# Second cross attention: TensorE takes a column's edge (x, result, logits, coefficients) between the projections and the attention's turn, instead of at the column's end

## The reference, cut to what matters

```python
def _L1_xattn_ref(q, k, v, Wq, Wk, Wv, Wo):     # 16 heads of 8 features, k = ctx_1024
    qp = q @ Wq.T
    kp = k @ Wk.T
    score = jnp.einsum('bldn,bmdn->blmn', qh, kh) / jnp.sqrt(jnp.float32(HEAD_DIM))
    attn = jax.nn.softmax(score, axis=2)
    x = jnp.einsum('blmn,bmdn->bldn', attn, kh)     # the keys serve as values
    return x.reshape(b, l, DIM) @ Wo.T

def _route(x, router_w, e_bias):                # first step of the experts' block
    scores = jax.nn.sigmoid(x @ router_w.T)
    sfc = scores + e_bias[None, :]
    ...                                         # the 4 best of 8 groups, in them the 8 best experts
    w = jnp.take_along_axis(scores, topk_idx, axis=1)
    w = w / (w.sum(-1, keepdims=True) + 1e-20)
    return (topk_idx, w * SCALE)

x = _layernorm(x + _L1_xattn_ref(x, ctx_1024, ctx_1024, ...))
x = _layernorm(x + _L1_ffn_ref(x, ...))         # coefficients of 64 experts for each token
```

## Time and profile before

| what | value |
|---|---|
| median of three runs | 3888.11 us (3886.36 to 3895.16) |
| the profiled execution, its own time | 3876.06 us |
| span of the profile, first to last instruction | 3874.2 us |
| PE busy | 3391.5 us, 88% |
| DVE busy | 2991.6 us, 77% |
| ACT busy | 2401.0 us, 62% |
| POOL busy | 1889.9 us, 49% |
| this phase, 2290 to 2825 us: PE, DVE, ACT busy | 411.23, 405.12, 330.52 us of 535 |
| this phase, granted PE clock | 0.84 of full speed |

### The profile page before, as it was taken

How to read it: one execution, slowest core, us unless ns; L and a number is a source line. 1 busy time by engine, 2 the same in 40 slices (tenths; PEclk the granted TensorE clock), 3 DMA queues, 4 the chain that set the end, 5 groups by cost and what they waited for, 6 DMA issues and landing times. The chain is left out here.

```text
span 3874.2 us, 92251 instructions
## 1 busy us (share of the span) xinstructions
PE 3391.5 (88%) x30917; PEld 2192.8 (57%) x30917; DVE 2991.6 (77%) x6170; ACT 2401.0 (62%) x5410; POOL 1889.9 (49%) x2387
## 2 busy tenths in 40 slices
PE   6899999999685883799999977888789999999998
PEld 3466666666454782566666656777534444444443
DVE  6777777777584663798999957888868888888887
ACT  1355555556683442698999966766546565656565
POOL 1000000000473663677777743333268888888887
PEclk9999999999897876798999979898799999999999
DMA  2000000000122222000000012222176666666663
GB/s 85 7 10 9 11 9 9 11 9 10 52 60 70 58 61 39 19 17 18 18 18 18 16 29 61 72 75 73 49 152 145 141 144 141 144 140 144 141 144 85
DMA packets 285207, 243.72 MB, mean 63 GB/s; under 512 B 58472, under 2 KB 212236, under 8 KB 285068
## 3 DMA queue, kind: packets, MB, share of 16 engines
q1 hardware_dynamic: 273676, 237.22, 25.5%
q10 hardware_dynamic: 11392, 4.79, 0.5%
HBM read 210.34 MB, written 31.59 MB: 62 GB/s over the span
## 5 line engine op out<-in xcount | busy, mean ns | idle before, releaser
L2660 POOL TENSOR_TENSOR d_hidden<-d_gated,d_upper 128x512 f32<-128x512 f32 x528 | 812.5, 1564 | 177.7 <-DVE d_upper L2781 89.0
L2788 DVE TENSOR_TENSOR d_h_low<-d_hidden,d_h_high 128x512 f16<-128x512 f32 x528 | 543.9, 1030 | 120.4 <-ACT d_h_high L2736 118.6
L2730 ACT ACTIVATE d_gated<-d_g 128x512 f32<-128x512 f32 x528 | 314.6, 596 | 395.0 <-PE d_u L2676 395.0
L750 POOL MEMSET f_minus_half<- 128x4 f32 x1 | 0.1, 101 | 864.5 <-POOLq L37 864.5
L2781 DVE TENSOR_TENSOR d_upper<-d_u,d_coef 128x512 f32<-128x512 f32 x512 | 348.5, 681 | 33.1 <-DMA d_coef<-coefT 19.3
L1825 ACT ACTIVATE c_sc<-c_sc,c_negmax 128x129 f32<-128x129 f32 x1024 | 326.3, 394 | 9.2 <-issue 4.2
L2736 ACT ACTIVATE d_h_high<-d_hidden 128x512 f16<-128x512 f32 x528 | 328.3, 622 | 5.0 <-POOL d_hidden L2660 5.0
L1653 POOL TENSOR_TENSOR c_posg<-w_pos,c_gate 128x512 f32<-128x512 f32 x256 | 265.9, 1039 | 0.0
L1732 PE MATMUL c_turned<-all_ident,c_sc 128*128 128x128 f32 x1024 | 184.1, 307 | 33.7 <-ACT c_sc L1825 33.3
L2674 PE MATMUL d_g<-d_x_high,w_W_high 128*128 128x512 f16 x528 | 200.6, 380 | 11.2 <-POOL d_x_low L2653 8.2
L2674 PE MATMUL d_o<-d_h_high,w_W_high 128*128 128x512 f16 x528 | 200.1, 379 | 2.1 <-ACT d_h_high L2736 1.7
(11 more groups left out here) (407 smaller groups left out, 9685.6 us busy)
## 6 DMA issues: line engine op xcount, KB each, us to landing
d_coef<-coefT SPq DMA_DIRECT2D x256, 512.0 KB, 7.1
d_cT<-in_ctxT SPq DMA_DIRECT2D x128, 64.0 KB, 2.0
d_stage<-in_moe_W SPq DMA_DIRECT2D x48, 128.0 KB, 2.1
mx_x<-in_xT SPq DMA_DIRECT2D x16, 256.0 KB
b_x<-in_x SPq DMA_DIRECT2D x64, 64.0 KB
y<-b_y SPq DMA_DIRECT2D x64, 64.0 KB, 1.6
f_y<-y SPq DMA_DIRECT2D x16, 256.0 KB, 3.4
f_x<-in_x SPq DMA_DIRECT2D x16, 256.0 KB, 3.6
```

The costliest lines, as they stand in the source:

```text
L2660: nc.gpsimd.tensor_tensor(hidden[b][:], gated[b][:], upper[b][:], ALU.mult).then_inc(h_ready, 1)
L2730: nc.scalar.activation(gated[b][:], ps_g[i][:], ACT.Silu, scale=1.0 / W_SCALE).then_inc(silu_ready, 1)
L2788: nc.vector.tensor_tensor(h_low[b][:], hidden[b][:], h_high[b][:], ALU.subtract).then_inc(h_low_ready, 1)
```

## The change

PE takes the edge after `project` and before `turn_attn`. The diff is whole:

```diff
--- before.py
+++ after.py
@@ -2281,12 +2281,12 @@
                     run(scores, beside(it, j, 0))
                     run(weigh, beside(it, j, -1))
                     run(project, beside(it, j, 1))
+                    if beside(it, j, 2) or beside(it, j, -COEFS):
+                        edge(it, j)
                     run(turn_attn, beside(it, j, -1))
                     run(turn_e, beside(it, j, 0), 0)
                     run(turn_e, beside(it, j, 0), 1)
                     run(output, beside(it, j, -1))
-                    if beside(it, j, 2) or beside(it, j, -COEFS):
-                        edge(it, j)
                 pipelined(nc.tensor, column)
```

## The result

The changed kernel takes 3932.57 us (median of four runs, 3928.27 to 3938.70); the kernel before, four runs, 3890.88 us (3886.36 to 3895.16). The ratio is 1.0108 with a 95% interval of 1.0089 to 1.0128: slower by 42 us, between 35 and 50. The forecast was 3922 in a range of 3904 to 3943.

A forecast was written before the change was run, and what follows sets the result against it. A chain passing between engines, none full, was taken to bound the columns. The moved wait's +38.2 and the low clock's -4 gave +34 us, on the 3888.1 us median 3922 us, range 3904 to 3943.

The forecast's parts named there:

- case A: The forecast itself: full price of the moved wait with varying low-clock costs, +25 to +51 us; chance 0.74.
- the moved wait: In fourteen coefficient columns, both attention turns now queue behind the wait for DVE's coefficients: +38.2 us.
- The two terms on the clock, -4 and 0: Low-clock columns gain 4 us from the edge's move; a clock falling oftener adds nothing, 10 us kept for the range.
- rival B: Low clock on one column's projections per period, the edge delaying turn and scores by 1.1 us: +59, 3947 us; chance 0.12.
- The coefficients' time does not depend on the order: In coefficient columns, DVE's coefficients come 7.89 us after the scores, whatever PE does in between.
- The wait's price: Coefficient columns last 10.88 us instead of 8.15, +2.73 each, +38.2 us over fourteen.
- Plain columns at nothing: In plain columns the edge's 0.5 us fits PE's idling ahead of the attention's turn: 0 to 0.1 us, taken as zero.
- Columns at the low clock, -4 us: In columns at 1.2 GHz, moving the edge from the end saves more than it costs ahead of the turn: -4 us.
- A clock that falls oftener, 0 with 10 for the range: PE's longer coefficient wait may leave turns and scores behind it at 1.2 GHz: nothing extra, 10 us for the range.
- The result's wait: The edge's wait for ACT's norm of tile c-2, latest in `choose` columns, is covered by DVE's chain: costs nothing.
- C: The column behind a coefficient column gives back 1.14 us through ACT's earlier edge copy: +18, 3906 us; chance 0.10.
- D: Coefficients ready before the projections end, so the edge passes without waiting: faster, about 3866 us; chance 0.04.

The follow-up runs named there:

- e2: The change applied in coefficient columns alone, the edge keeping its old place elsewhere; 3929.56 us against 3880.75 before, ratio 1.0135.
- e1: The change in every column except coefficient columns, where the edge keeps its old place at the end; 3894.11 us against 3880.75 before, ratio 1.0041.
- e3: The changed kernel with the coefficients turned one column later (tile c-11 instead of c-10); 3904.05 us, ratio 1.0063 to the kernel before.
- e4: The kernel before, edge late, with the coefficients turned one column later; 3889.89 us, ratio 1.0024 to the kernel before.
- e10: e1 with 10 turns of the identity on PE at the end of all but coefficient columns; 3884.19 us against 3886.58 before, ratio 0.9994.
- e5: The changed kernel with 24 turns of the identity on PE in its wait for the coefficients; 3935.13 us, ratio 1.0112 to the kernel before.
- e6: The kernel before with 12 turns of the identity on PE in its wait for the coefficients; 3880.24 us against 3887.38, ratio 0.9976.

## Why the prediction was right, and which step failed

The forecast was +34 us, measured are +42 (35 to 50): the medians lie in case A's span and in the range. The main term, the moved wait, was right in mechanism and size. The rest was partly luck. The two terms on the clock, -4 and 0, were both too low, the sign that I had named for rival B appeared, and the total stayed near the forecast because the `choose` columns gave back 10.8 us that I had not foreseen. Step by step:

**The coefficients' time does not depend on the order.** Forecast 7.89 us after the scores, measured 7.86 in a column that begins at the full clock. Right.

**The wait's price.** Forecast +2.73 us a column, 10.88 long: 0.2 us to the turn and 2.79 from there. Measured 11.01 instead of 8.19 on average, +2.82; in the column shown 0.18 to the turn and 3.01 from there. The second is between the 2.79 of the full clock and the 3.08 of the low one, since PE came out of the wait at 1.2 GHz (the turned exponentials took 1.91 us). 14 columns give 39 us where I had 38.2. Right; e2 shows this term alone, with what follows from it (the column behind at 8.16 instead of 7.08): 49 us. One sign was off: I had expected the 16 waits to come to some 60 us of 4 us or more each, and they are 52.8 us, of 3.9 at most where scores are computed (one of 9.9 stands behind the last scores, before and after the change), because PE often came to them late at the low clock.

**Plain columns at nothing.** Right at the full clock: the edge's first step starts 3.38 us after the scores, the attention is turned at 4.00 to 4.01, and such a column lasts 6.79 us, as before. The cover that I named is just long enough.

**Columns at the low clock, -4 us.** This is the step that failed. I took the gain at the column's end (0.42) against a loss ahead of the turn (0.2 to 0.4), from one `choose` column in which DVE had left PE 0.60 us of idling. In the columns where the low clock covers weighing and projections there is no idling: there the edge delays the turn by nearly its whole 0.96 us, and what is saved at the end is swallowed by the wait for ACT. I had such a column at hand and gave its price, +1.1, to rival B alone. I also missed that the weighing slows from 1.83 to 3.20 us; a column with both (8.56 us) was in the trace of before and not looked at. e1 and the pair e3 and e4 measure what the early place costs without the wait: +13 and +14 us in place of -4. Corrected by this the sum is 38 + 13 = 51, above the measured 42 and its interval, and under the 58 of the traces.

**A clock that falls oftener, 0 with 10 for the range.** This term was too low as well. The clock fell oftener (0.79 against 0.87), and in every second period the column behind the coefficients was slow throughout, 9.9 us. The three other kinds of column together took 14.9 us more over 13 periods (+18.6 behind the coefficients, +7.1 next, -10.8 in `choose`); the early place at the low clock, the term above, is in this too. Rival B's mechanism was thus at work in every second period, and there it cost 2.8 us (9.91 against 7.08) where B had 1.1 in each: the mean period of 34.2 us with a granted clock of 0.79 is the sign I had named for B (over 34, well under 0.87). B's total of +59 was not reached in the medians, though the two traces differ by 58.

**The result's wait.** Costed at nothing, measured 1.2 us in all, 0.2 at most: right.

**C and D** are out: the column stayed over 10 us, and nothing came back behind it at the full clock. D's condition, that the coefficients pass without waiting, was made by e3 with a later turn; its gain was mostly eaten by the early place and ACT's gaps.

**The 16 us between traces and medians.** A single trace of this kernel is one draw of where the low clock falls: the periods of the kernel before took from 29.4 to 31.7 us in one execution, and its runs span 3870 to 3892 us on one chip and 3871 to 3897 on another. I had compared medians in the end, which was right, but took the size of the low-clock surplus from one of the faster executions. How much of the 16 us this explains was not measured.

Left open: what exactly makes the clock fall in this phase, and why ACT stands still five times in the experts' loop of the kernels with a later turn.

## What to carry to other kernels

When a group of steps is moved up in an engine's queue, look for the one among them that waits in only some of the rounds: it takes all that it is moved past into its wait, and a step that fits its new gap in the usual round can still cost several times its length in the others. Size the gap in the worst state that the trace holds (here the low clock, where gap and idle time vanish together), not in a clean column. And measure variants of an order in the same batch of runs with a trace each: in e4 a loss of 9 us in the total hid a gain of 12 in its phase and a loss of 23 in code that was not touched.

## What was not expected of the hardware

- With the coefficients turned one column later, ACT paused five times for 4.5 to 6.7 us in the experts' loop, one phase further on, with nothing in the trace that it waited for; 27 to 30 us in all, in five kernels of five, and in none of those with the old lag.
- The same 32 matmuls of the weighing took 1.83 us at 2.4 GHz and 3.20 at 1.2, though each moves only 18 columns.
- The clock fell from 1.00 to 0.50 both in a wait of 3.9 us and, at about 2610 us of the changed kernel, in a stretch of PE work that had not idled since 2607.03. Turns of the identity in idle time raised the granted clock from 0.85 to 0.95 (e10), but in e5 a filled wait only moved the fall to the next column, while in e6 it raised the clock from 0.87 to 0.92.
